# Self K and V weights loaded into the place of the weight sums, first self tile's scores and exponentials in the cross block

## What is computed

```python
x = x + cross_attention(_layernorm(x), ctx_1024, mask)   # 16 heads of 32, rotary by position, scale 64**-0.5
x = x + self_attention(_layernorm(x))
x = x + experts(_layernorm(x))

# self_attention
qkv = hidden_states @ c_attn_kernel.T + c_attn_bias
q, k, v = jnp.split(qkv, 3, axis=2)                      # 16 heads of 32
bias = jnp.where(causal, 0.0, neg)
scores = jnp.einsum('bqhd,bkhd->bhqk', q * scale, k) + bias
attn_weights = jax.nn.softmax(scores, axis=-1)
attn_output = jnp.einsum('bhqk,bkhd->bqhd', attn_weights, v)
out = attn_output @ c_proj_kernel.T + c_proj_bias
```

## Time and profile before

| | |
|---|---|
| median of 3 runs | 777.29 us (777.06 to 777.75) |
| the profiled execution | 776.16 us, span 774.3 us |
| TensorE busy | 739.7 us (96%) |
| VectorE, ScalarE, GpSimd busy | 560.2, 408.4, 345.6 us |
| cross block | 0 to 541.4 |
| self block, tiles 1 to 7 | 541.4 to about 655 |
| routing, experts, sum | from about 655 to the end |

### The profile page before, as it was taken

One profiled execution on the slowest core, in us unless ns is written; L12 is line 12 of the kernel. 1 busy time (PEld: TensorE's weight loads), 2 busy tenths in 40 slices (PEclk: granted clock), 3 DMA queues, 4 the chain that ended last, 5 costly groups with the idle time before them and its releaser, 6 DMA issues. The chain is left out here.

```text
span 774.3 us, 23209 instructions
## 1 busy us (share of the span) xinstructions
PE 739.7 (96%) x9494; PEld 646.1 (83%) x9495; DVE 560.2 (72%) x1293; ACT 408.4 (53%) x930; POOL 345.6 (45%) x364
## 2 busy tenths in 40 slices
PE   8999999999999999999999999997899999599997
PEld 7888889999899989988989989985677777478884
DVE  6786786967868768778697696755888998812236
ACT  5445466565566556555656556553566665133330
POOL 1664455456456545655545545521132221246640
PEclk9999999999999999999999999999999999789999
DMA  8310301121101011010120110133943238634538
GB/s 287 142 35 23 118 2 58 64 69 58 38 28 56 9 57 58 9 56 6 54 64 2 57 64 2 57 110 109 366 195 136 96 124 321 219 124 172 183 130 325
DMA packets 23317, 78.99 MB, mean 102 GB/s; under 512 B 3344, under 2 KB 4752, under 8 KB 20144
## 3 DMA queue, kind: packets, MB, share of 16 engines
q1 hardware_dynamic: 19536, 65.50, 23.6%
q0 software_dynamic: 3680, 12.06, 4.7%
HBM read 58.93 MB, written 18.61 MB: 100 GB/s over the span
## 5 line engine op out<-in xcount | busy, mean ns | idle before, releaser
L1356 PE MATMUL bank<-ctx_parts_hi,wparts 128*128 128x258 f32 x224 | 67.2, 300 | 0.7 <-DVE ctx_parts_lo L890 0.7
L890 DVE TENSOR_TENSOR ctx_parts_lo<-craw,ctx_parts_hi 128x1032 fp32r<-128x1032 f32 (+1 forms) x56 | 63.2, 1129 | 2.7 <-ACT ctx_parts_hi L626 2.6
L1357 PE MATMUL bank<-ctx_parts_hi,wparts 128*128 128x258 f32 x224 | 63.3, 283 | 0.0
L1358 PE MATMUL bank<-ctx_parts_lo,wparts 128*128 128x258 f32 x224 | 63.3, 282 | 0.0
L1383 PE MATMUL bank<-wparts,ctx_parts_hi 128*128 128x256 f32 x224 | 63.1, 282 | 0.0
L1381 PE MATMUL bank<-wparts,ctx_parts_hi 128*128 128x256 f32 x224 | 62.9, 281 | 0.0
L1384 PE MATMUL bank<-wparts,ctx_parts_lo 128*128 128x256 f32 x224 | 62.9, 281 | 0.0
L657 ACT ACTIVATE v<-bank 128x512 f32<-128x512 f32 x56 | 33.2, 594 | 52.8 <-PE bank L1384 52.3
L475 POOL TENSOR_TENSOR ksin<-kb_even,const 128x258 f32<-128x258 f32 (+1 forms) x42 | 46.7, 1112 | 31.5 <-ACT kb_even L647 30.2
L661 ACT ACTIVATE wraw<-wraw,nmax 128x257 f32<-128x257 f32 x96 | 47.9, 501 | 22.8 <-DVE nmax L983 21.0
L1356 PE MATMUL bank<-ctx_parts_hi,w_sums_hi 128*128 128x258 f32 x168 | 52.0, 309 | 0.6 <-DVE wraw L962 0.4
(11 more groups left out here) (413 smaller groups left out, 2623.6 us busy)
## 6 DMA issues: line engine op xcount, KB each, us to landing
craw<-ctx_t_dram SPq DMA_DIRECT2D x32, 516.0 KB, 4.3
expert_lo<-weights_dram SPq DMA_DIRECT2D x8, 1024.0 KB, 12.2
expert_hi_scratch<-wraw SPq DMA_DIRECT2D x16, 512.0 KB, 2.6
wparts<-expert_hi_scratch SPq DMA_DIRECT2D x8, 1024.0 KB, 8.9
wraw<-weights_dram SPq DMA_DIRECT2D x6, 1024.0 KB, 4.9
expert_lo<-ffn_out_scratch SPq DMA_DIRECT2D x16, 256.0 KB, 5.5
x<-x_dram SPq DMA_DIRECT2D x8, 256.0 KB, 4.4
craw<-weights_dram SPq DMA_DIRECT2D x2, 1024.0 KB, 5.0
```

Of the source, the lines that this page charges most:

```text
L890: dve.tensor_tensor(dst[1], src, dst[0].bitcast(F32), ALU.subtract).then_inc(s_clo, 1)
L1356: pe.matmul(psum, whi_i[:, i, cols], hi[:, i, :], start=own and i == 0, stop=False, skip_group_check=not own)
L1357: pe.matmul(psum, wlo_i[:, i, cols], hi[:, i, :], start=False, stop=False, skip_group_check=not own)
L1358: last = pe.matmul(psum, whi_i[:, i, cols], lo[:, i, :], start=False, stop=i == 1, skip_group_check=not own)
```

## The change

What it moves and adds:

- `w_sums_hi` and `w_sums_lo` share their place with a new buffer `late_weights_raw` of two weights. Self K and self V weights are loaded there, both as soon as V product 5 of the last pair is done; before, K waited for the low parts of self Q and V for the rotary products of step 31. Biases wait for the low parts of Q instead of K.
- Step 30: ScalarE makes V copy 6 ahead of the attention part of step 29 and the exponentials, the high parts of self K weights behind the probability copies, and of self V weights behind the last V copy. VectorE takes the statistics of tile 1 between two V sums and makes the low parts of both weights at the end. TensorE makes self Q of tile 0 in two halves, one on each side of V product 4.
- Step 31: VectorE normalises tile 1, adds the biases to Q and K of tile 0, transposes them by batches, and makes the low parts of tile 1's rows. TensorE makes tile 1's transposes (into bank 0, once Q has left it) and self V ahead of the diagonals, and Q of tile 1 and the scores of tile 0 behind the attend. ScalarE makes tile 0's key blocks. Behind the last step VectorE masks the scores, takes and subtracts the maxima and ScalarE takes the exponential. To have room, the self tiles take the place of cross tiles (`kb_even`, `kcos` and `ksin` as `k_trig`, `v0`, `qb`, `qt0`, `vlast`), each with a wait on the last reader.
- Self block: body 0 is gone on ScalarE and VectorE; body 1 has no Q product, no scores of tile 0 and no `stay_awake` on TensorE, and makes the high and low parts of the output projection weights.

The core of the diff:

```diff
@@ sync
-                    if n == AK:
-                        sp.wait_ge(s_wlo, AQ)
-                    if n == AV:
-                        sp.wait_ge(s_kcos, trig_of(B - 1))
-                        sp.wait_ge(s_ksin, trig_of(B - 1))
+                    if n in (AK, AV):
+                        sp.wait_ge(s_vp1, v_product_of(PAIR_LAST, 5))
...
-                sp.wait_ge(s_wlo, AK)
+                sp.wait_ge(s_wlo, AQ)
@@ scalar, even_step
+                    if not more:
+                        v_copy(p, 6)
                     before_o_hi(b)
                     exp(b, 0)
                     exp(b, 1)
-                    v_copy(p, 6)
+                    if more:
+                        v_copy(p, 6)
...
+                    if not more:
+                        w_hi(AK)
                     v_copy(p, 4)
...
                     else:
-                        w_hi(AK)
+                        act.wait_ge(s_vp1, v_product_of(PAIR_LAST, 4))
+                        w_hi(AV)
@@ scalar, behind the last step
-                o_hi(B - 1, TILES - 1, BT - 1)
                 act.wait_ge(s_xtp, TILES + 2)
                 act.wait_ge(s_vp, 1)
-                act.activation(xthi[:], bank[3][:]...).then_inc(s_xthi, 1)
+                act.activation(xthi[:], bank[0][:]...).then_inc(s_xthi, 1)
+                self_k_blocks()
+                o_hi(B - 1, TILES - 1, BT - 1)
+                act.wait_ge(t_msub, 1)
+                act.activation(self_sm, self_sm, ACT.Exp, scale=A_SCALE).then_inc(t_exp, 1)
@@ vector
                     if not more:
                         w_lo(AK)
+                        w_lo(AV)
...
                 def last_step(b, j):
                     begin_step(b, j)
+                    self_ln_apply()
+                    self_evac(0)
                     o_sum(b - 1)
                     inverse_sums(b)
                     pair_parts(b)
+                    self_evac(1)
+                    self_k_by_batch()
                     o_lo(b - 1, (b - 1) % BT)
-                    ln(TILES + 1, x[:, 1, :])
-                    w_lo(AV)
+                    self_q_by_batch()
+                    self_xt_lo()
...
                 o_sum(B - 1)
+                self_evac(2)
                 o_lo(B - 1, BT - 1)
+                self_scores_less_max()
@@ tensor
-                        self_product(0)
+                        self_product(0, part=range(2))
                     v_product(p, 4)
+                    if not more:
+                        self_product(0, part=range(2, KC))
...
                 def last_step(b, j):
                     self_product(1)
                     probs_transposed(b)
+                    self_xn_transposed()
+                    self_product(2)
                     diagonals_spread(b)
                     attend(b, j)
+                    self_product(0, t=1)
+                    self_scores()
...
-                self_product(2)
-                pe.wait_ge(s_xn, TILES + 2)
-                for c in range(KC):
-                    last = pe.transpose(bank[3][:, c * P:(c + 1) * P], xn[:, c * P:(c + 1) * P], ident)
-                last.then_inc(s_xtp, 1)
                 out_product(TILES - 1, B - 1)
@@ tensor, self block
                 def body(t, depth=2, last=False):
-                    qkv_product(t, 0)
                     if depth >= 2:
+                        qkv_product(t, 0)
                         probs_transposed(t - 1)
-                        qkv_product(t, 1)
-                    if depth == 1:
-                        qkv_product(t, 1, range(2))
-                        scores(t - 1)
-                        qkv_product(t, 1, range(2, KC))
-                    qkv_product(t, 2)
+                    qkv_product(t, 1)
                     if depth == 1:
                         probs_transposed(t - 1)
-                        stay_awake(b_cp, 3)
+                    qkv_product(t, 2)
                     attend(t - 1)
```

More of the change, by code:

```diff
@@ L245, in perceiver @@
             self_raw = craw_both[:].rearrange("p i c n -> p (i c n)")[:, 0:KC * D].rearrange("p (c n) -> p c n", n=D)
+            late_raws = [late_raw[:, i, 0:KC * D].rearrange("p (c n) -> p c n", n=D) for i in range(2)]
             def raw_of(n):
-                return self_raw if n in (AQ, AK) else wraw[n % 2][:]
+                return {AQ: self_raw, AV: late_raws[0], AK: late_raws[1]}.get(n, wraw[n % 2][:])
             def w_block(w, i):
@@ L851, in last_step, with self_k_blocks @@
                         exp(b, g)
-                    before_o_hi(b)
                     for g in range(G):
                         pt_evac(b, g)
-                    act.wait_ge(s_vp1, v_product_of(PAIR_LAST, 4))
-                    w_hi(AV)
+                    before_o_hi(b)
+                def self_k_blocks():
+                    act.wait_ge(t_kt, 1)
+                    act.wait_ge(s_sc, B)
+                    for i in range(BT):
+                        last = act.activation(self_kbd.rearrange("p h (b n) -> p h b n", b=BT)[:, :, i, :], self_kt, ACT.Copy,
+                                              scale=const[:, C_HMS + i:C_HMS + i + 1])
+                    last.then_inc(t_kbd, 1)
                 for b in range(B):
@@ new lines, in self_evac @@
+                def self_evac(u):
+                    dve.wait_ge((s_qp, s_kp, s_vp)[u], 1)
+                    if u == 0:
+                        dve.wait_ge(s_bias2, 32)
+                        dve.wait_ge(s_ksin, trig_of(B - 2))
+                    elif u == 1:
+                        dve.wait_ge(s_av, B - 1)
+                    else:
+                        dve.wait_ge(s_qtp, 2 * TILES)
+                    dve.tensor_tensor(self_qkv[u], bank[u][:], self_bias[u], ALU.add).then_inc((t_qsb, t_ksb, t_vsb)[u], 1)
@@ L1445, in self_product, with self_xn_transposed, self_scores @@
                     w = SLOT[AQ + u]
-                    mm3(pe, bank[u][:], lambda c: xthi[:, c, :], lambda c: xtlo[:, c, :],
-                        lambda c: whi[w][:, c, :], lambda c: wlo[w][:, c, :]).then_inc((s_qp, s_kp, s_vp)[u], 1)
+                    last = mm3(pe, bank[u][:], lambda c: xthi[:, c, :], lambda c: xtlo[:, c, :],
+                               lambda c: whi[w][:, c, :], lambda c: wlo[w][:, c, :], part=part)
+                    if part[-1] == KC - 1:
+                        last.then_inc((s_qp, s_kp, s_vp)[u], 1)
+                def self_xn_transposed():
+                    pe.wait_ge(s_xn, TILES + 2)
+                    pe.wait_ge(t_qsb, 1)
+                    for c in range(KC):
+                        last = pe.transpose(bank[0][:, c * P:(c + 1) * P], xn[:, c * P:(c + 1) * P], ident)
+                    last.then_inc(s_xtp, 1)
+                def self_scores():
+                    pe.wait_ge(t_kbd, 1)
+                    pe.wait_ge(t_qt, 1)
+                    pe.wait_ge(s_pt, B * G)
+                    for h in range(H):
+                        rows, cols = slice(h % 4 * S, h % 4 * S + S), slice(h // 4 * P, h // 4 * P + P)
+                        last = pe.matmul(quad[rows, 0, cols], self_qt[:, h, :], self_kbd[:, h, :], start=True, stop=True)
+                    last.then_inc(t_sc, 1)
                 def v_last_product():
@@ L1742, in perceiver, with qkv_bank @@
             LAST_OUT = ((slice(0, D // 2), 6), (slice(D // 2, D), 3))
-            def qkv_bank(t, u):
-                return b_x3 if u == 0 and isinstance(t, int) and t == 1 else (b_q, b_k, b_v)[u]
+            def qkv_bank(u):
+                return (b_q, b_k, b_v)[u]
             sum_bank = (b_score, b_av, b_v, b_xt, b_k, b_q, b_cp, b_x3)
@@ L1974, in body @@
                         x3_evac(t - 2)
-                body(0, depth=0)
                 body(1, depth=1)
@@ L2516, in qkv_product @@
                         pe.wait_ge(s_xtlo, TILES + t + 1)
-                    if part[0] == 0 and not (t == 1 and u == 0):
+                    if part[0] == 0:
                         pe.wait_ge((s_qsb, s_ksb, s_vsb)[u], t)
                     w = SLOT[AQ + u]
-                    last = mm3(pe, qkv_bank(t, u), lambda c: xthi[:, c, :], lambda c: xtlo[:, c, :],
+                    last = mm3(pe, qkv_bank(u), lambda c: xthi[:, c, :], lambda c: xtlo[:, c, :],
                                lambda c: whi[w][:, c, :], lambda c: wlo[w][:, c, :], part=part)
```

135 lines of the change are left out of this document (78 added, 57 removed).

## The result

The changed kernel took 774.76 us in the median of 12 runs (773.27 to 777.33), the kernel before, on the same chip, 776.57 in 12 (775.63 to 782.4). The ratio, which rests on all these runs, is 0.9967, 95% interval 0.9952 to 0.9981: 0.33% or some 2.6 us faster. The two medians differ by 1.8 us, the means by 2.4. The forecast was 3.2 us less, 774.1. The profiled execution took 774.37 us, span 772.6, against 776.16 and 774.3 of before.

What follows compares the result with a forecast made beforehand. Bound: the chain of waits through the seam between blocks, via expert loads and ScalarE, with TensorE full behind it. Opening -4.56 plus clock 1.35 gives -3.2 us; median 777.29 becomes 774.1, range 772.0 to 776.0.

Steps and rivals of the forecast that it cites:

- Steps 30 and 31, the opening: End of the cross block: it ends, and the second block opens, 4.56 us earlier, plus or minus 0.8.
- The V copy: Step 30, ScalarE: V copy 6 goes ahead of the exponentials, so V product 7 starts at 511.95, not 512.92.
- The masking: Step 31, VectorE: masking, behind both low parts, starts at 522.1 against 524.43; added wait 1.2 us.
- The giving back: Second block: ScalarE waits for eight expert loads, landed 561.9; of 12.9 us won, 8.3 turn into a wait.
- the stall: TensorE ahead of the attend of tile 1: idle from 558.25 to 566.15, 7.9 us.
- The clock: After TensorE's idle wait: 1.2 GHz at once, full clock back after 4.8 us, scores of tile 2 end 1.35 us late.
- one of the signs that I had named of being wrong: Wrong if opening under 3 us earlier, a body over 15.4 us, or no idle before attend of tile 1.
- the tail: Behind 573: no slack to hide or add to it, but routing's clock recovery can move by a microsecond either way.
- A: Rival: no clock loss after the wait, or a somewhat earlier opening; -4.6 to -5.4 us, 772.3; chance 0.10.
- B: Rival: last cross steps don't shrink as laid out, opening held at 2 us earlier; -0.6 us, 776.7; chance 0.12.
- C: Rival: clock stays low some 14 us, through attend to tile 3's products; +1.9 us, 779.2; chance 0.06.
- D: Rival: the change does all it says and the expert loads don't gate; -12 us, 765; chance 0.02.

Runs made afterwards that it cites:

- a1_after: The changed kernel with no edit, profiled in a second execution; 774.19 us, ratio 0.9957 to the kernel before.
- c3_after: The changed kernel with no edit, run and profiled a third time; 775.36 us, ratio 0.996 to the kernel before.
- a4_vcopy: The changed kernel with V copy 6 of the last pair back between the exponentials of step 30; 775.37 us, ratio 0.9967 to the kernel before.
- b1_before: The kernel before with no edit, profiled in a second execution; 778.34 us, ratio 0.9993 to the kernel before.
- a3_awake: The changed kernel with 13 extra matmuls on TensorE in its stall ahead of the attend of tile 1; 774.53 us, ratio 0.9952 to the kernel before.
- a2_split: The changed kernel, ScalarE's first expert conversion waiting for the first two expert loads alone, not eight; 767.53 us, ratio 0.9862 to the kernel before.
- b4_late_loads: The changed kernel with the waits of the self K and V weight loads put back as before; 780.91 us, ratio 1.0035 to the kernel before.
- c2_vcopy_before: The kernel before with only V copy 6 of the last pair put ahead of step 30's exponentials; 778.04 us, ratio 0.9982 to the kernel before.

## Why the prediction was right

**Steps 30 and 31, the opening.** Forecast 4.56 us earlier, measured 4.35 from the mark. The V copy was to bring 0.97 and brought 1.03. The masking was to start at 522.1, 14.92 behind the mark; it started at 524.52, 14.79 behind. V product, attend, Q of tile 1 and the one idle time on VectorE's low parts (0.45 forecast, 0.55 measured) are where they were put. That the end of the block would be a tie of TensorE and ScalarE came out: the exponential ended at 539.19 and the block opened 0.4 later.

**The giving back.** Right in mechanism and place. The loads landed at 564.70, which is 54.97 behind the mark, forecast 54.7 (561.9). The term that was mis-sized is the stall: 6.4 us, not 7.9. Its end was right within 0.4 (569.09 is 59.36 behind the mark, forecast 58.97), its start was not: tile 2's products ended at 562.7, some 1.9 later than forecast, since the self tile ahead of them had 0.24 and 0.54 of idle time that I had not seen, the opening was 0.2 late, and the rest is some tenths a product. This cost nothing: it only made the stall shorter.

**The clock.** I put the fall "at once"; it came some 3.5 us into the stall (0.55 for 566 to 568 is about 1.8 us at half). The recovery was put 4.8 us after work resumed. It came 3.9 behind it in after and a1_after, 5.3 in c3_after and 5.1 in a4_vcopy, where the stage behind the opening is 0.7 us longer. The loss was put at 1.35; against the kernel that kept the clock up it was 0.95 in the first two and 1.7 in c3_after. So the forecast lies between what executions of one kernel show, and that the row used for it, one execution's, came out in the middle is luck. The whole stage behind the opening is 1.2 longer than in before (119.86 against 118.63); had the trace of before been like b1_before (119.69), it would have been 0.2. The Trainium skill, TensorE: Matmul & The Clock Gate, section Part 1: The HAM clock gate, has a stall on DMA paid for twice; the trace agrees, with a second price of a seventh to a quarter of the first (0.95 to 1.7 beside stalls of 6.4 to 6.6).

**What the sum left out.** Three terms of about 1 us each. The new places of the tensors slow the cross block by 0.4 to 1.2 us, ahead of all that I looked at; I had costed moving tensors at nothing without a word. They also brought the bodies to 15.39 to 15.41 us, the edge of one of the signs that I had named of being wrong (over 15.4). And the stall of 3.25 us, which the change removes, costs the kernel before more in some executions (0.7 in b1_before) than in the one that I read. And the tail, which the forecast kept unchanged to a microsecond either way, was 1.1 us shorter in after than in before (114.28 to 113.15), with 3.4 us less at the low clock in routing: the granted clock from 682 to 686 was 0.66 in before and 0.97 in after. Such a shorter low stretch is in a1_after too and not in c3_after, whose tails are alike all the same (113.80, 113.82), and in one of the five profiles of the old order. Whether the change makes it likelier is open. The first term works against the other two, so that 3.2 us forecast and 2.6 to 3.3 measured agree better than the sum deserves. Part of the closeness of 774.1 to 774.76 is luck as well: the kernel before stood at 776.57 in the runs beside it, not at 777.29.

**The base.** I set the profiled execution 1.1 us under the median of the runs. Its missing dip at 40 us, worth about 1, is of that size; that it is the reason is not shown, since the runs without a profile have no trace. The two ranges of the forecast, 3.8 to 5.4 and 0.4 to 2.4, add up to -5.0 and -1.4 at their ends, not -4.9 and -1.6.

**The rivals.** A (no clock loss) is out by the clock of 0.50 and by a3_awake. B (the last steps don't shrink) by the openings at +29.86, +29.87 and +29.88. C (a clock low for 14 us) by the full clock from 573.0 (6.8 us at the low level, 3.9 of them under work). D (the loads don't gate) by a2_split.

## What to carry to other kernels

A wait in an in-order queue that isn't last today, such as one for eight loads where two are read, becomes the bound as soon as the work around it is made faster: split such waits by what the next instruction reads, when the change is made and not after. Before comparing two traces of a long kernel, align them at the last mark ahead of the change, and compare stages; chance and the new places of tensors had moved the traces apart by 2.5 us here, about as much as the change was worth. And a reordering that needs data earlier is worth something only together with the earlier load: here the new order with the old loads opened the second block 5.8 us later than with the early ones, and 0.8 to 1.5 us later than the old order.

## What the runs showed of the hardware that I had not expected

- TensorE's granted clock fell to half for 3.4 us at about 41 to 45 us in 10 of 13 profiles and for 6.8 us in one, though TensorE had been busy without a gap since about 24; in two it did not. Each fall of 3.4 us cost 1.1 us at once (in after the lag was 0.12 at 36 us and 1.25 at 50), of which some 0.2 to 0.3 was gone again by 80 us.
- The place of tensors in SBUF alone, with the same instructions in the same order, moved matmul sequences by 0.03 to 0.06 us at a time and a body of the self block by 0.02 to 0.05; the kernel's time moved by 0.15% (interval 0 to 0.31%).
- A store of 512 KB, issued 14 us behind the first of the eight loads of 1 MB, took 12.0 us to land where the median of the 16 such stores in that trace is 2.6, and ScalarE waited 2.84 us for it in a2_split. By the loads' own time in after (23.6 us from the first issue) that is some 2.5 us behind the last of them.
- The one load of 1 MB in b4_late_loads, with the biases right behind it in the queue, took 4.9 us, and the eight in a row 23.6, 2.95 each. My expectation took the second price for the first.
- Around the same stall of 3.25 us in the same place, the granted clock was at 0.50 for 3.4 us in three profiles of the old order and for 6.8 us in two (b1_before, c2_vcopy_before), which cost 0.7 us more in b1_before.
